# Merging expert rows by token on TensorE and adding them into a DRAM table, instead of 128 mask matmuls

## The reference

```python
xn = _layernorm(x)
x = x + _L1_attn_ref(xn, ...) + _L1_ffn_ref(xn, ...)
# _L1_ffn_ref: 32 experts, each token goes to its 4 best, 32 slots per expert (CAP)
xe = zeros((E, CAP, h)).at[sel, posc].add(x[tok] * valid)      # dispatch
g = silu(einsum('ech,ehf->ecf', xe, Wg)); u = einsum('ech,ehf->ecf', xe, Wu)
ye = einsum('ecf,efh->ech', g * u, Wd)
y_pair = ye[sel, posc] * (w * valid)                            # weight per slot
out = shared.at[tok].add(y_pair)                                # back to the tokens
# shared = silu(x @ Wsg) * (x @ Wsu) @ Wsd * sigmoid(x @ Wse)
```

## Time and profile before

| | us |
|---|---|
| median of 3 runs | 428.7 (428.68 to 429.19) |
| profiled execution, its own time | 429.21 |
| its span, first to last instruction | 426.8 |
| PE busy in the span | 419.8 (98%) |
| DVE / ACT / POOL busy | 310.9 / 247.5 / 168.6 |
| granted TensorE clock | 1.00 throughout |

### The profile page before, as it was taken

The page is one execution under the profiler, slowest core; times in us unless marked ns, Lnnn a source line. Parts: engine busy times, 40 slices in busy tenths (PEclk is TensorE's granted clock), DMA queues, the critical chain, the costliest instruction groups (busy, mean ns, idle before and its releaser), DMA issues.

```text
span 426.8 us, 8853 instructions
## 1 busy us (share of the span) xinstructions
PE 419.8 (98%) x3070; PEld 377.2 (88%) x3070; DVE 310.9 (73%) x910; ACT 247.5 (58%) x671; POOL 168.6 (40%) x293
## 2 busy tenths in 40 slices
PE   8999999999999999999999999999999999999997
PEld 8788879999999999999999999999997777567797
DVE  5967575787787888787877767657689994688442
ACT  4666741887868788777867786434314622563120
POOL 3520002645554554554554530102077007699200
DMA  7800020501010101010000000000099942899002
GB/s 214 303 2 1 2 76 25 198 1 51 2 51 0 51 2 51 2 52 1 2 0 3 2 2 0 27 14 12 26 321 300 307 115 88 236 305 279 9 14 86
DMA packets 37754, 34.45 MB, mean 81 GB/s; under 512 B 2448, under 2 KB 35920, under 8 KB 37712
## 3 DMA queue, kind: packets, MB, share of 16 engines
q1 hardware_dynamic: 37328, 32.85, 26.2%
q0 software_dynamic: 384, 1.05, 0.8%
HBM read 31.80 MB, written 2.10 MB: 79 GB/s over the span
## 4 chain that ended last, share of the span: by engine, by line
PE 92%; DVE 5%; ACT 2%; issue 1%; POOL 0%; POOLq 0%; DVEq 0%
PE bank L945 21%; PE bank L947 21%; PE bank L946 21%; PE bank L1116 5%; PE bank L1128 3%; PE bank L1107 3%; PE bank L1350 2%; PE bank L1317 2%; PE bank L1361 2%; PE bank L1362 2%; PE bank L1158 2%; PE bank L1337 2%; DVE OS L1859 1%; PE bank L1022 1%; PE bank L1266 1%; DVE arena L1499 1%
## 5 line engine op out<-in xcount | busy, mean ns | idle before, releaser
L587 POOL TENSOR_TENSOR arena<-arena,rinv 128x384 f32<-128x384 f32 x64 | 52.9, 828 | 81.0 <-DVE rinv L1629 81.0
L945 PE MATMUL bank<-XTl,WA 128*128 128x512 f32 (+1 forms) x126 | 52.0, 412 | 0.9 <-DVE arena L1499 0.8
L947 PE MATMUL bank<-XTh,WA 128*128 128x512 f32 (+1 forms) x126 | 49.1, 390 | 0.0
L946 PE MATMUL bank<-XTh,WA 128*128 128x512 f32 (+1 forms) x126 | 49.1, 389 | 0.0
L771 ACT ACTIVATE PT<-bank 128x256 fp32r<-128x256 f32 x64 | 24.5, 383 | 34.0 <-PE bank L1116 34.0
L1633 DVE TENSOR_TENSOR PT<-bank,PT 128x256 fp32r<-128x256 f32 x64 | 27.2, 425 | 18.8 <-ACT arena L772 18.8
L945 PE MATMUL bank<-WA,XTh 128*128 128x256 f32 x128 | 38.3, 299 | 0.0
L578 POOL CAST Q<-arena 128x128 fp32r<-128x128 f32 x64 | 18.7, 292 | 47.0 <-PE bank L947 47.0
L946 PE MATMUL bank<-WA,XTl 128*128 128x256 f32 x128 | 35.7, 279 | 0.0
L947 PE MATMUL bank<-WA,XTh 128*128 128x256 f32 x128 | 35.7, 279 | 0.0
L1621 DVE CUSTOM_DVE_ANT_0 arena<-bank,posm 128x128 f32<-128x128 f32 x64 | 18.1, 283 | 20.8 <-PE bank L947 20.8
(11 more groups left out here) (329 smaller groups left out, 1455.5 us busy)
## 6 DMA issues: line engine op xcount, KB each, us to landing
arena<-in_L_ffn_Wg SPq DMA_DIRECT2D x6, 704.0 KB, 7.8
arena<-in_L_ffn_Wu SPq DMA_DIRECT2D x6, 704.0 KB, 10.3
arena<-in_L_ffn_Wd SPq DMA_DIRECT2D x6, 512.0 KB, 7.2
arena<-in_L_attn_Wk SPq DMA_DIRECT2D x8, 256.0 KB, 2.6
arena<-in_L_attn_Wv SPq DMA_DIRECT2D x8, 256.0 KB, 3.2
arena<-in_L_attn_Wo SPq DMA_DIRECT2D x1, 2048.0 KB, 8.4
arena<-in_L_ffn_Wd SPq DMA_DIRECT2D x6, 192.0 KB, 7.6
arena<-in_L_attn_Wq SPq DMA_DIRECT2D x4, 256.0 KB, 4.7
```

Source lines behind the costliest of these rows:

```text
L587: pool.tensor_tensor(pr, pr, r[:, :, None].to_broadcast([P, 3, P]), ALU.mult).then_inc(s_p, 1)
L945: pe.matmul(dst, wh, xl, start=start, stop=False)
L946: pe.matmul(dst, wl, xh, start=False, stop=False)
L947: return pe.matmul(dst, wh, xh, start=False, stop=stop)
```

## The change

The mask matmuls of groups 0 to 6 go. In their place, each group's 128 rows are first merged by token: a 128 x 128 matrix `SAME[g]` with a 1 where two slots of the group hold the same token is multiplied with the weighted rows, so that every slot of a token holds the token's whole sum of that group (`expert_merge`, one plain fp32 matmul per group). ACT copies this to SBUF, and POOL adds the 128 rows into a DRAM table `expert_rows` of 1152 rows with an indirect DMA that accumulates. The row places `rank` send the first slot of each token to the token's row and later slots of the same token to spare rows behind row 1024, so that no row is named twice in one DMA. Each such scatter waits for the landing of the one before. When the seventh has landed, SP loads the table back in four DMAs into `YS`, and DVE adds it to `X`. Group 7 keeps its mask, one `GT`, and two matmuls per tile. The table is zeroed at the start by one DMA of 1152 rows.

With this, `shared_down` has two PSUM banks instead of three, the attention's last tile of values moves from POOL to DVE (`last_values`), and the value transposes are split in two halves (`ao`) between the last groups' steps.

```diff
+                 ... ("up", 3), ("ranks", 0), ("merge", 0), ("down", 1), ("turn", 2), ("sd", 1), ("merge", 1), ...
+                 ("down", 5), ("values", 0), ("turn", 6), ("sd", 5), ("merge", 5), ("down", 6), ("up", 7), ("values", 1), ("merge", 6), ("sd", 6),
+                 ("turn", 7), ("ao", 0), ("down", 7), ("ao", 1), ("sd", 7), ("add", 7)]
+PV_STEPS = [("values", 0, 0, 1), ("values", 1, 0, 1), ("values", 2, 0, 2), ("scatter", 0), ("values", 3, 0, 2), ("scatter", 1),
+            ("values", 4, 0, 3), ("scatter", 2), ("values", 5, 0, 3), ("scatter", 3), ("values", 6, 0, 2), ("scatter", 4),
+            ("values", 6, 2, 4), ("scatter", 5), ("scatter", 6)]
...
@@ sync: after the first key and value load; at the end
+            sp.dma_start(expert_rows.rearrange("(g p) d -> p g d", p=P), ZR[:, None, :].to_broadcast([P, GR + 1, D])).then_inc(s_xs, 16)
...
+            sp.wait_ge(s_xg[LAST - 1], 32)
+            for k in range(B):
+                sp.dma_start(YS[:, 2 * k:2 * k + 2], expert_rows[2 * P * k:2 * P * k + 2 * P].rearrange("(g p) d -> p g d", p=P)).then_inc(s_x[k], 16)
@@ gpsimd
+            pool.wait_ge(s_gt, 2)
+            pool.affine_select(out=BEFORE, in_=SAME[:, 0:LAST], compare_op=ALU.is_gt, fill=0.0, base=0,
+                               pattern=[[0, LAST], [-1, P]], channel_multiplier=1).then_inc(s_it, 1)
...
+            def scatter(g):
+                if g == 0:
+                    pool.wait_ge(s_rk, 1)
+                else:
+                    pool.wait_ge(s_xg[g - 1], 32)
+                pool.wait_ge(s_yr, g + 1)
+                pool.indirect_dma_start(expert_rows, bass.IndirectOffsetOnAxis(ap=rank[:, g:g + 1], axis=0), YZ[:, g % 2], None,
+                                        compute_op=ALU.add).then_inc(s_xg[g], 16)
@@ scalar
-            def y_high(n):
-                act.wait_ge(s_ye, n + 1)
-                nc.scalar.activation(YH[:, n], YE[:, n], ACT.Copy, scale=slot_w[:, n:n + 1]).then_inc(s_yr, 1)
+            def y_weighted(g):
...
+                nc.scalar.activation(YW[:, g % 2], pb[7][:, 0:D], ACT.Copy, scale=slot_w[:, g:g + 1]).then_inc(s_ye, 1)
+            def y_merged(g):
+                act.wait_ge(s_mg, g + 1)
+                if g >= 2:
+                    act.wait_ge(s_xg[g - 2], 32)
+                nc.scalar.activation(YZ[:, g % 2], pb[3][:, 0:D], ACT.Copy).then_inc(s_yr, 1)
@@ tensor
+                for half in range(2):
+                    ins = pe.matmul(pb[4 + half][:], onesr[0:1, :], TKr[0:1, 512 * half:512 * half + 512], start=True, stop=True)
...
+            def expert_merge(g):
+                pe.wait_ge(s_ye, g + 1)
+                if g >= 1:
+                    pe.wait_ge(s_yr, g)
+                pe.matmul(pb[3][:, 0:D], SAME[:, g], YW[:, g % 2], start=True, stop=True).then_inc(s_mg, 1)
...
-            def mix_groups(j, groups, start, stop):
-                dst, ts = mix_tile(j)
-                for g in groups:
-                    pe.matmul(dst, GT[g][:, ts], YH[:, g], start=start and g == groups[0], stop=False)
-                    ins = pe.matmul(dst, GT[g][:, ts], YL[:, g], start=False, stop=stop and g == groups[-1])
+            def final_tile(j):
+                dst, ts = pb[FINAL_BANK[j]][:, 0:D], slice(P * j, P * j + P)
+                for c in range(C):
+                    mm3(dst, AOTh[:, c, ts], AOTl[:, c, ts], PJh[:, c], PJl[:, c], c == 0, False)
+                pe.matmul(dst, GT[:, ts], YH[:], start=False, stop=False)
+                pe.matmul(dst, GT[:, ts], YL[:], start=False, stop=True).then_inc(s_fo, 1)
@@ vector
+            def same_token(half):
+                n = 4 if half == 0 else LAST - 4
+                dve.wait_ge(s_tt, 2 + half)
+                nc.vector.scalar_tensor_tensor(out=SAME[:, 4 * half:4 * half + n], in0=pb[4 + half][:, 0:P * n]..., scalar=1.0,
+                                               in1=slot_t[:, 4 * half:4 * half + n, None].to_broadcast([P, n, P]), op0=ALU.max, op1=ALU.is_equal)
+            def row_places():
+                dve.wait_ge(s_it, 4)
+                nc.vector.tensor_reduce(earlier[:], BEFORE, AX, ALU.add)
...
+            def add_rows(j):
+                dve.wait_ge(s_x[j // 2], 32)
+                step(nc.vector.tensor_tensor(X[:, j], YS[:, j], X[:, j], ALU.add))
```

More of the change, by code:

```diff
@@ L243, in program @@
         pvt = sb("pvt", [P, 256])
-        s_x = [sem(f"x_loaded{b}") for b in range(B)]
+        onesr = sb("onesr", [1, P], FR)
+        spare = sb("spare", [P, 1])
+        earlier = sb("earlier", [P, LAST])
+        slot_d = sb("slot_d", [P, LAST])
+        rank = sb("rank", [P, LAST], U32)
+        expert_rows = nc.dram_tensor("expert_rows", (N + P, D), F32, kind="Internal").ap()
+        s_x = [sem(f"x_then_expert_rows_loaded{b}") for b in range(B)]
         s_xb0 = sem("x_second_tile_loaded")
@@ new lines, in scatter @@
+            def scatter(g):
[6 more added lines that the diff above has]
+                                        compute_op=ALU.add).then_inc(s_xg[g], 16)
+            for what, *n in PV_STEPS:
+                if what == "values":
+                    values(*n)
+                if what == "scatter":
+                    scatter(*n)
@@ L925, in _ @@
                     nc.scalar.activation(ACTh[:, n - 1], ACTT[n - 1][:, N // 2:N], ACT.Copy).then_inc(s_adh, 1)
-                if what == "high":
-                    if n == 0:
[L928 to L938, removed]
+                if what == "down":
+                    y_weighted(n)
+                if what == "merge":
+                    y_merged(n)
+                if what == "ao":
+                    if n == 0:
+                        nc.scalar.activation(PJh[:], projT[:], ACT.Copy).then_inc(s_pjh, 1)
+                    for c in range(C):
+                        act.wait_ge(s_at, 2 * n + c + 1)
+                        nc.scalar.activation(AOTh[:, c, 512 * n:512 * n + 512], pb[ao_bank(c, n)][:], ACT.Copy).then_inc(s_ac, 1)
         @block.tensor
@@ L1597, in fill_copy @@
                     dve.wait_ge(s_xb, NT)
+                    dve.wait_ge(s_xs, 16)
                 if f < 4:
@@ new lines, in last_values @@
+            def last_values(part):
+                j = NT - 1
+                for k in (0, 1) if part == 0 else (2, 3):
+                    dst = AO[:, j] if k == 0 else pvt2
+                    p, v = value_operands(j, k)
+                    step(nc.vector.tensor_tensor(dst.rearrange("p (g r d) -> p g r d", g=G1, r=4), p, v, ALU.mult))
+                    if k:
+                        ins = nc.vector.tensor_tensor(AO[:, j], AO[:, j], pvt2, ALU.add)
+                        if k == 3:
+                            ins.then_inc(s_pd, 1)
+                        else:
+                            step(ins)
@@ L1874, in _ @@
                     shared_product(n[0])
+                if what == "shared" and n == (11, 1):
+                    same_token(0)
+                    same_token(1)
                 if what == "table":
@@ L1900, in _ @@
                 if what == "mask":
-                    for g in n:
-                        dve.wait_ge(s_it, 4)
-                        slot_mask(g)
-                if what == "low":
-                    for g in range(n, n + 3):
-                        y_low(g)
+                    dve.wait_ge(s_it, 5)
+                    nc.vector.tensor_scalar(GT[:], IT, slot_t[:, LAST:GR], None, ALU.is_equal).then_inc(s_gt, 1)
                 if what == "sd" and n >= 1:
```

219 lines of the change are left out of this document (122 added, 97 removed).

## The result

| | us |
|---|---|
| changed kernel, median of 6 runs | 431.67 (429.99 to 433.17) |
| kernel before, beside it | 429.09 (428.68 to 430.08) |
| ratio, 95% interval | 1.0054 [1.0028, 1.0079] |
| profiled execution, own time / span | 430.82 / 428.7 |
| forecast | 419.3, range 416.3 to 431.0 |

In 12 later runs, with 23 of the kernel before beside them, the ratio was 1.0032 [1.0019, 1.0045]. By the two ratios the change costs 1.4 to 2.3 us, and the time is 0.7 us above the upper end of the range.

The account below looks back on a forecast made before the run. PE, busy 419.8 of 426.8 us, was the bound; its net -11.6 us gave 417.6. The scatter chain ended 2.2 us later, 419.8 on the profiled scale, so 419.3 us forecast, range 416.3 to 431.

Parts of the forecast that it names:

- What PE loses: On PE near the end: 128 mask matmuls at 0.118 us, 15.1 us, and a 0.4 us wait go; net -11.6 us.
- What PE gains: On PE: group 7's 16 matmuls 1.9 us, seven merges 1.5 us, two slot-table broadcasts 0.5 us.
- Work that others take on, the weights: Added DVE, ACT and POOL work costed at nothing; last weights delayed to 399 us, hidden with 2 us to spare.
- The chain's start: On POOL: scatter 0 starts at about 372 us, after group 3's `up` and DVE's row places.
- L in the saturated stretch: Time from a scatter's issue to its landing while weights of groups 4 to 7 load: taken as 5.0 us.
- L in the quiet stretch: Time from a scatter's issue to its landing once DMA is quiet: taken as 4.0 us.
- The five intervals: Between starts of scatters 0 to 5 on POOL: 5.0, 5.6, 5.6, 5.0 and 4.7 us, together 25.9.
- the queue argument: DMA engines alternate between queues by packet, so POOL's scatters would not stand behind SP's weights; landing nearer the quiet one.
- The intervals' rule: Each interval between scatters is the larger of the landing time and 1.1 us issue plus POOL's values at 0.9 each.
- The end: After scatter 6 lands at 406.1 us: loads to 411.2, row adds 412.1, final adds 415.3, tail 2.1, span 417.4.
- Rival 2: Change slower: seven scatters back to back, landings above 6.3 us, POOL and ACT held; 434.9 us at 7; chance 0.16.
- Rival 3: DVE holds up scatter issues on POOL, some 1.3 us each, five make 6.7 us; time 422 to 427; chance 0.15.

Follow-up runs that it names:

- experiment 1: Changed kernel without the seven scatters, the table's reload and the row adds; merges and copies stay: 419.29 us, ratio 0.9788 to the kernel before.
- experiment 3: Weight loads of groups 4 to 7 dropped: from the changed kernel 426.39 us, ratio 0.9948; from the kernel before 428.19 us, ratio 0.9996.
- experiment 4: Changed kernel with seven buffers for merged rows instead of two, so ACT waits for no landing: 432.68 us, ratio 1.0087 to the kernel before.

## Why the prediction was wrong, step by step

- **What PE loses**: right, as far as the net shows. Without scatters PE had no wait, and its last start moved from 423.88 to 414.17, by 9.7 us of the 11.6 forecast (experiment 1); the next item has the rest.
- **What PE gains**: mis-sized by 1.9 us. Seven merges cost 3.5 us, not 1.5, because the 12 rows are 6 matmuls. So PE's bound is a span of 417.1, not 415.2.
- **Work that others take on, the weights**: right, at nothing, for the engines' work. DVE and ACT had room, and PE waited for no weights.
- **The chain's start**: 373.45 instead of 372, 1.4 us late.
- **L in the saturated stretch**: this is the step that failed. I took 5.0 us; the three landings took 7.7, 6.3 and 7.4. L in the quiet stretch, 4.0, was right: 3.74 to 3.96. The five intervals took 33.4 us instead of 25.9, and all of the 7.5 us lies in the first three (8.4 + 7.1 + 8.2 against 5.0 + 5.6 + 5.6). Of it 5.2 us are the landings, and 2.3 us the handover from a landing to the next issue, 0.7 to 0.8 us each, which my rule for these intervals put at nothing. I had the row that says so, 8.0 us for a plain store of the same size among weights, used it as the upper end, and let the queue argument draw the value down towards the gather's 2.8, a row measured at a DMA share of 0.31 (352.4 to 362.5 us of the kernel before). Of the eight stores of that row, two stood among weights, and landed after 8.0 and 6.7 us.
- **The intervals' rule**, the larger of L and (1.1 + values): an accumulating issue costs 1.6, not 1.1, and the handover comes on top of L. At equal landings, values and issue would still have given 8.0 us once (experiment 3).
- **The end**: from scatter 6's landing to the span's end I had 11.3 us (406.1 to 417.4); it took 13.5 (415.15 to 428.7). Loads 0.5 more, four row adds left instead of two, and the stores could not go out beside PE's work, so the tail was 3.3 instead of 2.1.
- **The sum** of the offsets: 1.4 + 7.5 + 0.1 + 0.5 + 1.0 - 0.4 + 1.2 = 11.3 us, from the forecast span of 417.4 to 428.7.

Rival 2 came true in its mechanism: POOL, ACT and PE were held, in that order. It held for three links of six only; with L at 6.3 to 7.7 in these and below 4 in the rest, the time stayed far from the 434.9 that it had for L = 7 throughout. I gave it 0.16. Rival 3 is seen only where the chain is not late. In the kernel with two tables the second scatter's issue started 0.4 us behind a 1.76 us DVE instruction with two SBUF inputs and took 2.85 us; the other issues there took 1.6 to 1.7:

```profile
377.41 1.76 DVE L2016 TENSOR_TENSOR SDl<-FRF,SDh 128x1536 fp32r<-128x1536 f32 x1 [4.17 <-ACT SDh L987]
```

```profile
377.78 2.85 POOL L688 DMA_INDIRECT odd_rows<-arena,rank  x1 [0.28 <-POOL arena L678]
```

The Trainium skill (SBUF — State Buffer, Who interferes with whom) says that a DVE instruction with two SBUF inputs contends with a GpSimd instruction that reads SBUF; the issue, which reads the row places `rank` from there, agrees, at about 1.2 us. In the changed kernel no issue met that instruction, so it cost nothing there. The gathers did not run beside a nearly idle DVE, as I wrote: it was busy 5.0 of the 10.1 us from 352.4 to 362.5, but with short instructions of at most 0.7 us. The other rule, round-robin by packet between queues (the Trainium skill, DMA: Bandwidth & Descriptors, Queues, rings and completion order), did not give what I drew from it: a scatter from POOL's queue landed twice as late while SP's queue was full of weights, 7.7 us for the first against 3.8 in the quiet kernel.

What stays open: how much of the doubled landing is reading, writing or the queue, since no row splits a landing. A scatter of plain writes had intervals of 6.3 to 7.6 there, so it isn't the addition alone. And no run has both the quiet DMA engines and values off POOL, so how far the single table can come is not shown.

## What to carry to other kernels

When matmuls are traded for a chain of DMAs, price each link with a row that was taken under the traffic in which it will run, and multiply by the number of links that wait for one another. Then ask who stands behind the waiting instruction: here POOL's values and ACT's copies, whose release moved the wait but not the end. What helped was to cut the chain (two tables, every second landing) and to let the end's adds and stores run beside PE; the saved matmuls then showed as time.

## What was not expected of the hardware

- An accumulating scatter of 128 rows of 1 KB has an issue of 1.57 to 1.74 us on POOL, a plain one 0.98 to 1.23. It made 144 packets, a plain scatter and a gather 48 each (1392 packets on the software queue, 720 with plain scatters, 384 without scatters).
- With the weights on the way it landed after 6.3 to 7.7 us, without them after 3.7 to 4.6; some 0.5 to 0.8 us more passed until POOL issued the next one that had waited for it.
- PE's clock went to its lower level for 3.4 us after waits of 2.4 and 1.2 us, and for 6.8 us in the second profile of the changed kernel; without the waits (experiments 1 and 4) the same stretch ran at 1.00.
